# First attention of an eight-layer block: the first mixture's rows are gathered inside it

## The reference, cut to what matters

```python
x = x + mamba(layernorm(x))
x = x + ffn0(layernorm(x))      # mixture of 32 experts, 4 of them for each token
x = x + attn_b(layernorm(x))    # "rotary": 16 heads of 16, causal
x = x + ffn0(layernorm(x))
x = x + attn_sinks(layernorm(x))
x = x + ffn1(layernorm(x))      # mixture of 48 experts, 8 for each token
x = x + attn_latent(layernorm(x))
x = x + ffn1(layernorm(x))
```

```python
def ffn0(x):                    # its end
    outs = experts(x)[inverse_order].reshape(-1, 4, 256)
    return sum(outs * topk_weight[..., None], axis=1)

def attn_b(x):
    q, k, v = split(x @ w_atten.T)          # 16 heads of 16
    q, k = rope(q), rope(k)
    att = softmax(where(causal, q @ k.T / 4, -inf))
    return (att @ v) @ w_proj.T
```

## Time and profile before

| | us |
|---|---|
| median of 3 runs | 4055.43 |
| lowest and highest | 4052.91, 4055.51 |
| span of the profiled execution | 4055.4 |

### The profile page before, as it was taken

How to read it: one execution, slowest core, us unless ns; L and a number is a source line. 1 busy time by engine, 2 the same in 40 slices (tenths; PEclk the granted TensorE clock), 3 DMA queues, 4 the chain that set the end, 5 groups by cost and what they waited for, 6 DMA issues and landing times. The chain is left out here.

```text
span 4055.4 us, 68591 instructions
## 1 busy us (share of the span) xinstructions
PE 3283.2 (81%) x19700; PEld 2595.3 (64%) x19707; DVE 2809.6 (69%) x6227; ACT 2274.5 (56%) x5958; POOL 1766.8 (44%) x3039
## 2 busy tenths in 40 slices
PE   7799967925888489169999999999957499999575
PEld 3355556714777377058778778778745378888453
DVE  5699966646777666368858858768673378888742
ACT  3599923414777344068858868768602166666211
POOL 0299923567664045635535445446327400000165
PEclk9699977967999689579999999999956599999666
DMA  2011132440000335310000000000053500000435
GB/s 86 20 47 47 49 153 80 137 104 24 1 1 1 148 99 136 98 59 19 19 9 19 20 9 20 17 10 20 16 184 63 119 1 1 1 1 1 160 72 111
DMA packets 139453, 221.35 MB, mean 55 GB/s; under 512 B 28912, under 2 KB 114800, under 8 KB 137408
## 3 DMA queue, kind: packets, MB, share of 16 engines
q1 hardware_dynamic: 108432, 156.23, 11.6%
q0 software_dynamic: 30720, 61.44, 7.3%
HBM read 162.60 MB, written 54.80 MB: 54 GB/s over the span
## 5 line engine op out<-in xcount | busy, mean ns | idle before, releaser
L1242 POOL DMA_INDIRECT ex_xr<-scratch_rows,mo_token x288 | 287.0, 997 | 326.1 <-PE bank L1301 167.7
L596 POOL TENSOR_TENSOR sc_h<-sc_h,sc_c 128x512 f32<-128x512 f32 x256 | 327.0, 1291 | 198.1 <-DVE sc_h L633 190.1
L3034 DVE TENSOR_TENSOR sa_pT<-bank,sa_pT 128x512 fp32r<-128x512 f32 x512 | 329.9, 686 | 34.4 <-ACT sa_pT L2902 30.5
L2894 ACT ACTIVATE sa_p<-bank,sa_nm 128x512 f32<-128x512 f32 x512 | 347.0, 689 | 2.5 <-DVE sa_nm L3025 2.5
L633 DVE TENSOR_TENSOR_SCAN sc_h<-sc_da,bank 128x512 f32<-128x512 f32 x256 | 311.1, 1220 | 39.4 <-ACT sc_da L576 24.5
L2723 PE MATMUL bank<-sa_kT,sa_qT 128*128 128x512 f32 x1024 | 332.5, 436 | 1.5 <-DVE residual L3001 1.5
L3021 DVE TENSOR_REDUCE sa_mx<-bank 128x2 f32<-128x1024 f32 x256 | 312.4, 1220 | 25.7 <-PE bank L2725 22.0
L1319 PE MATMUL bank<-mo_w_gu,ex_xT 128*128 (+2 forms) x1152 | 315.7, 403 | 1.1 <-issue 0.5
L2747 PE MATMUL bank<-sa_pT,sa_v 128*128 128x256 f32 x2048 | 301.5, 290 | 16.9 <-DVE sa_pT L3034 16.5
L2747 PEld LDWEIGHTS bank<-sa_pT,sa_v 128*128 128x128 f32 x2048 | 260.2, 190 | 40.1 <-DVE sa_pT L3034 31.6
L2902 ACT ACTIVATE sa_pT<-bank 128x512 fp32r<-128x512 f32 x512 | 274.3, 585 | 7.9 <-PE bank L2735 0.7
(11 more groups left out here) (401 smaller groups left out, 9405.6 us busy)
## 6 DMA issues: line engine op xcount, KB each, us to landing
scratch_ys<-ex_yo SPq DMA_DIRECT2D x192, 128.0 KB, 2.1
mo_w_gu<-in_w_gu SPq DMA_DIRECT2D x2, 9216.0 KB, 26.8
sc_c<-scratch_c SPq DMA_DIRECT2D x64, 256.0 KB, 3.1
sa_share<-scratch_shares SPq DMA_DIRECT2D x256, 64.0 KB, 2.5
mo_w_dn<-in_w_dn SPq DMA_DIRECT2D x2, 4608.0 KB, 46.5
scratch_rows<-ln_stage SPq DMA_DIRECT2D x64, 128.0 KB, 1.9
mo_w_dn<-in_w_dn SPq DMA_DIRECT2D x2, 4096.0 KB, 34.8
ex_xr<-scratch_rows,mo_token POOLq DMA_INDIRECT x288, 2.8
```

The lines of the kernel that those rows point to most:

```text
L596: pool.tensor_tensor(h, h, C[u], ALU.mult).then_inc(used.sem, 1)
L1242: pool.indirect_dma_start(xr[u][:, :], None, rows, bass.IndirectOffsetOnAxis(ap=token[:, i:i + 1], axis=0), bounds_check=rows.shape[0] - 1 ...
L2894: act.activation(pr[h][:, :], SC[2 * s_ + h][:, :], ACT.Exp, bias=nm[:, col:col + 1], scale=SCALE, accum_out=rs[:, col:col + 1]).then_inc( ...
L3034: dve.tensor_tensor(spot(1), PT[h][:, :].rearrange("p (k n) -> p k n", k=TPB), spot(0).bitcast(F32), ALU.subtract).then_inc(*inc("kept_d"))
```

## The change

- After the first mixture there is no combine block. `slots` and `weights` are kept (`c.slots`, `c.weights`, in the scope `c.kept`) and `rotary` gathers and adds the rows itself. After the second mixture `combine(c)` runs as before, now as an entry of `LAYERS`.
- GpSimd, in the attention's block: first the 16 gathers of batch 0 (`fetch_rows`, 12 buffers `got`), then mask and identity, 8 gathers of batch 1, the rotation of all of group 1, the other 8 gathers of batch 1, and in the loop four gathers at the end of each of the groups 0 to 7.
- VectorE clears the `qT` parts (8 memsets) instead of GpSimd, then adds the 16 rows of batch 0, takes four statistics, and computes variance and deviation of batch 0 alone. In the loop it adds one row in each unit of group 0, one in every other unit of groups 3, 4, 7 and 8, and in groups 1, 5 and 9 it takes the next batch's statistics (`r` 0 to 3), its variance (`r` 3) and its deviation (`r` 6).
- VectorE rotates all four tiles of group 0, with `low_v(1, i)` after each; GpSimd none of them.
- ScalarE clears `vv` with four copies from zeros, and takes the root of batches 1 to 3 in the loop, at `r` 4 of groups 1, 5 and 9.

```diff
@@ rotary, GpSimd
+                fetch_rows(0, PB)
                 pool.memset(mask[:, :], 0.0).then_inc(*inc("made"))
...
-                for u in range(2):
-                    for hh in range(HG):
-                        rows = slice(WR, P) if hh % 2 == 0 else slice(0, WR)
-                        pool.wait_ge(*at("made", 4 + u * HG + hh))
-                        pool.memset(qT[u][rows, hh * SEQ:(hh + 1) * SEQ].bitcast(F32), 0.0).then_inc(*inc("made"))
-                for u in range(4):
-                    pool.memset(vv[u][:, :].bitcast(F32), 0.0).then_inc(*inc("made"))
-                pool.wait_ge(*at("made", 4 + 2 * HG + 4))
+                pool.wait_ge(*at("made", 4))
+                fetch_rows(PB, PB + 8)
...
-                put_group(0, (0, 1))
-                pool.sem_inc(sig["qput"].sem, 2)
+                pool.sem_inc(sig["qput"].sem, TPB)
                 put_group(1, range(TPB))
+                fetch_rows(PB + 8, 2 * PB)
                 for I in range(NG + 1):
...
+                    if 2 * PB + I * TPB < BATCH * PB:
+                        fetch_rows(2 * PB + I * TPB, 2 * PB + (I + 1) * TPB)
@@ rotary, TensorE
                     if I == 0:
-                        pe.wait_ge(*at("dput", 2))
+                        pe.wait_ge(*at("dput", TPB))
@@ rotary, ScalarE
+                for u in range(4):
+                    act.activation(vv[u][:, :].rearrange("p (o n) -> p o n", n=P),
+                                   blank.to_broadcast([P, TPB * HG + 1, P]), ACT.Copy).then_inc(v_cleared.sem, 1)
...
+                    if r == 4 and I % G == 1 and I // G + 1 < BATCH:
+                        take_root(I // G + 1)
@@ rotary, VectorE
+                def add_row(n):
+                    u, i = n % NB, n // K0
+                    at_x = c.x[:, i * D_MODEL:(i + 1) * D_MODEL]
+                    dve.wait_ge(fetched[u].sem, fetched[u].at(16 * (n // NB + 1)))
+                    if n % K0:
+                        dve.wait_ge(weighed.sem, weighed.at(n))
+                    dve.scalar_tensor_tensor(out=at_x, in0=got[:, u * D_MODEL:(u + 1) * D_MODEL],
+                                             scalar=c.weights[:, n:n + 1], in1=at_x,
+                                             op0=ALU.mult, op1=ALU.add).then_inc(weighed.sem, 1)
...
+                for i in range(TPB):
+                    for k in range(K0):
+                        add_row(i * K0 + k)
+                    if i >= 1:
+                        tile_stats(i - 1)
+                tile_stats(TPB - 1)
+                variance(0)
+                deviation(0)
...
-                for i in (2, 3):
+                for i in range(TPB):
                     dve.wait_ge(*at("qraw", i + 1))
                     st.then(put(dve, st, 0, i, scratch[1]))
                     dve.sem_inc(sig["dput"].sem, 1)
-                for i in range(TPB):
                     low_v(1, i)
...
+                    if I == 0:
+                        add_row(PB + r)
+                    if I % G in (3, 0) and r % 2 == 0 and PB <= (I + 1) // G * PB < (BATCH - 1) * PB:
+                        add_row(((I + 1) // G + 1) * PB + (I + 1) % G * (PB // 2) + r // 2)
+                    if I % G == 1 and I // G + 1 < BATCH:
+                        if r < TPB:
+                            tile_stats((I // G + 1) * TPB + r)
+                        if r == TPB - 1:
+                            variance(I // G + 1)
+                        if r == 6:
+                            deviation(I // G + 1)
@@ layers
-LAYERS = ["mamba", "moe0", "rotary", "moe0", "sinks", "moe1", "latent", "moe1"]
+LAYERS = ["mamba", "moe0", "rotary", "moe0", "combine", "sinks", "moe1", "latent", "moe1"]
```

More of the change, by code:

```diff
@@ L723, in moe @@
     TPBANK = TILES // EB
+    if which == 0:
+        keep = lambda name, dt: c.kept.enter_context(nc.sbuf_tensor(name, [P, TK], dt, allow_name_mangling=True))
+        c.slots, c.weights = keep("mo_slots", I32), keep("mo_weights", F32)
     with ExitStack() as s:
@@ L1091, in moe, with combine @@
             rowed[u].counted(16 * (TILES // 4))
[L1093 to L1097 removed]
+def combine(c):
     nc = c.nc
+    K, ROWS, ys, slots, weights = M0_K, M0_TILES * P, c.t["scratch_ys0"], c.slots, c.weights
     NB = 16
@@ L2096, in _, with fetch_rows @@
             def _(pool):
+                def fetch_rows(first, end):
+                    for n in range(first, end):
+                        u = n % NB
+                        if n >= NB:
+                            pool.wait_ge(weighed.sem, weighed.at(n - NB + 1))
+                        pool.indirect_dma_start(got[:, u * D_MODEL:(u + 1) * D_MODEL], None, ys,
+                                                bass.IndirectOffsetOnAxis(ap=c.slots[:, n:n + 1], axis=0),
+                                                bounds_check=ys.shape[0] - 1, oob_is_err=False) \
+                            .then_inc(fetched[u].sem, 16)
+                fetch_rows(0, PB)
                 pool.memset(mask[:, :], 0.0).then_inc(*inc("made"))
@@ L2380, in _ @@
-                st.then(dve.reciprocal(rstd[:, :], tmp[:, :]))
+                def add_row(n):
[7 more added lines that the diff above has]
+                                             op0=ALU.mult, op1=ALU.add).then_inc(weighed.sem, 1)
@@ new lines, in deviation @@
+                def deviation(b):
+                    cut = slice(b * TPB, (b + 1) * TPB)
+                    dve.wait_ge(*at("root", b + 1))
+                    st.then(dve.reciprocal(rstd[:, cut], tmp[:, cut]))
+                for u in range(2):
+                    for hh in range(HG):
+                        rows = slice(WR, P) if hh % 2 == 0 else slice(0, WR)
+                        dve.memset(qT[u][rows, hh * SEQ:(hh + 1) * SEQ].bitcast(F32), 0.0).then_inc(q_cleared.sem, 1)
+                for i in range(TPB):
[3 more added lines that the diff above has]
+                        tile_stats(i - 1)
@@ L2480, in rotary @@
             sig[n].counted(v)
+        for u in range(NB):
+            fetched[u].counted(16 * len(range(u, TILES * K0, NB)))
+        for q, v in ((weighed, TILES * K0), (q_cleared, 2 * HG), (v_cleared, 4)):
+            q.counted(v)
+    c.kept.close()
 def sinks(c):
```

61 lines of the change are left out of this document (36 added, 25 removed).

## The result

| | before | changed | ratio, 95% interval |
|---|---|---|---|
| median, us | 4055.47 | 4014.76 | 0.9896 (0.9882 to 0.9909) |
| lowest and highest of 4 runs | 4052.91, 4059.81 | 4010.83, 4016.94 | |
| span of the profiled execution | 4055.4 | 4008.8 | |

The account below looks back on a forecast made before the run. Gathers bound the combine, a VectorE chain the attention's start, VectorE-ScalarE hand-overs the loop. Saved 76.7, less 2.2 at the start and 30.2 in the loop, gives 44.3 us: 4055.4 to 4011 us, range 3996 to 4030.

Parts of the forecast that it names:

- What goes from the path: First gather to first normalized tile: 102.7 us shrinks to 26.0, saving 76.7 us.
- the clearing: Memsets moved to VectorE and ScalarE: first adds up to 2 or 3 us late, cost 0, at most 4.6 us.
- The start: Attention's start: VectorE's four rotations of group 0 delay the transposes by 3.7 us; net for this part 2.2 us.
- 1.5 back in group 0: Loop's group 0: TensorE's 1.49 us wait for GpSimd goes, as GpSimd starts group 1 earlier.
- one share, 0.78: Loop: 0.78 of 38.7 us added to VectorE and ScalarE is exposed, 30.2 us; ends 0.4 and 1.15.
- the added work is of the same kind and in the same places: Loop: the reason given for taking 0.78, from two groups differing by four normalizations, transposes and copies.
- The cost of 0: Loop: GpSimd's four gathers per group, 5.2 us, fit into its 8.1 us idle and cost nothing.
- its sign of being wrong: Loop: TensorE waiting for GpSimd's rotations would show the prediction wrong; no size given.
- A: Loop's idle time absorbs added work: 0.4 exposed or less, 3996 us or less, 3981 with nothing exposed; chance 0.08.
- B: Loop: more than all exposed through broken hand-overs, table loads and lower clock; 1.4 of 38.7, 4035 us; chance 0.08.
- C: Loop: slow gathers make GpSimd's rotations late; 4090 us at 4.5 us each, no gain above 3.4; chance 0.04.
- The two rules: Loop: a 1380 ns drain per table switch, 8.3 us over six, not counted; port lock, up to 3 us, put at nothing.

Follow-up runs that it names:

- e2_no_loop_rows: Changed kernel with the 48 gathers and 48 adds of batches 1 to 3 left out; 4003.71 us in one run.
- e1_copy_root: Changed kernel with ScalarE's square root of batches 1 to 3 replaced by a plain copy, so no table loads in the loop; 4004.09 us in one run.
- e12_no_variance: Changed kernel with the seven variance steps of batches 1 to 3 left out, mean 0 and variance 1 instead; 4005.66 us in one run.
- e7_newton: Changed kernel with loop adds moved into VectorE's waits and roots of batches 1 to 3 moved from ScalarE to VectorE and GpSimd; 4003.08 us, ratio 0.9872.
- e10_stats_placed: As e7_newton, with the loop's statistics put two and two ahead of the value copies of units 2 and 3; 3998.89 us, ratio 0.9863.
- e3_gathers_only: Changed kernel with the 48 adds of batches 1 to 3 left out but their 48 gathers made; 4001.95 us in one run.
- e11_stats_split: As e10_stats_placed, with GpSimd again rotating tiles 0 and 1 of group 0; 4011.67 us, ratio 0.9894.
- e8_pool_clears: Changed kernel with GpSimd again clearing both kinds of buffers, behind its first 16 gathers and the masks; 4021.7 us in one run.
- e9_changed_again: The changed kernel unaltered, run again on the chip of three other kernels; 4015.99 us, ratio 0.9902 against the kernel before.

## Why the prediction was right, and which steps failed

**What goes from the path: right.** 102.7 to 25.4 is 77.3 us; 76.7 was said. The gathers kept their pace, and nothing of the clearing, of the loads or of the tables added to it by the 16th add. The first adds were late by the 2 or 3 us that the prediction allowed, because the first row landed late, and not because of the clearing. The medians are those of the earlier trace rows; the longest gather took 1.18 us and the longest add 0.73:

```profile
L2113 POOL DMA_INDIRECT ra_got<-scratch_ys,mo_slots x64: 992/998/1176, 838.3 to 1107.2; - x64
L2403 DVE SCALAR_TENSOR_TENSOR residual<-ra_got,mo_weights,residual x64: 468/482/728, 843.5 to 1131.8; 128x256 f32<-128x256 f32 x64
...
DMA to landing us min/median/max: 2.7/2.8/5.2
```

**The start: a little short.** The forecast was 3.7 us later up to the first maximum, and 1.5 back in group 0. Measured: 4.6 and 5.3 later. VectorE's four rotations ran from 872.26 to 885.80 in the changed kernel, 13.5 us where 12.4 was said. (By the prediction's own numbers, 964.5 - 960.88, the first part is 3.6, not 3.7.) The 1.5 us did not come back although the wait for GpSimd in group 0 is gone: group 0 without its adds (e2_no_loop_rows) is 0.5 longer than before, not 1.5 shorter. Its first 4 us, and those of the kernel before:

```profile
892.20:896.20 4.00, 4.00 (x15) 3.49 (x15) 1.29 (x5) 2.63 (x10) 2.09 (x7) 0.50 0.01 4
```
```profile
966.00:970.00 4.00, 3.98 (x26) 3.16 (x25) 1.73 (x6) 2.78 (x11) 3.52 (x11) 1.00 0.02 4
```

TensorE is busy throughout in both, but does 15 matmuls at a granted clock of 0.50 in one and 26 at 1.00 in the other. It had stood idle for 5.7 to 6.1 us for the rotations. This cost of the longer wait stands in no step of the prediction. That it is what ate up the 1.5 us is the nearest reading; no run takes it away alone.

**The loop: the mechanism right, the share too small for one half of the work.** The sum has one share, 0.78, on 38.7 us: 30.2. With the 1.5 that was to come back the loop should have grown by 28.7; it grew by 35.9 and 37.3. By kind, from the runs:

| kind | added, us | cost of the loop, us | share |
|---|---|---|---|
| 48 adds | 19.9 | 15.2 to 15.6 | 0.76 to 0.78 |
| 6 table loads | 7.7 | 8.2 to 9.1 | 1.1 to 1.2 |
| 3 variances | 4.4 (5.9 measured) | 7.1 to 8.5 | 1.6 to 1.9 (1.2 to 1.4) |
| 48 gathers (GpSimd) | 62 of its time | 0.4 | 0 |
| the rest, not taken apart | 6.7 | 3 | 0.4 |

In the rows of loads and variances the lower cost counts groups 1, 5 and 9 alone. The kinds add up: in group 5 the loads make 2.8 us (e1_copy_root), the variance 2.6 (e12_no_variance) and the four statistics 1.3 (from e7_newton to e10_stats_placed), 6.7 together where the group took 6.6. The rest is 12 statistics, three reciprocals and three roots, together with what group 0 lost to the clock and won from the wait. The failing step is "the added work is of the same kind and in the same places". For the adds it was. The variance is seven dependent steps in one place ahead of one maximum, and the load holds up one exponential; such a block is longer than the wait that VectorE or ScalarE has in its one unit (1.4 us at most in the kernel before), so little of it is taken in, and TensorE runs at the lower clock behind it. A second step was mis-sized: the variance takes 1.98 us in the loop and not 1.46, 1.6 us over three batches. (Its 0.43 us for a statistic stands in no row shown, where the earlier trace rows give 0.49; it took 0.42.) The share was taken from normalizations that stand one to a unit, and must not be carried to a block.

**The gathers and GpSimd: right for the change, with less room than said.** The cost of 0 held, and its sign of being wrong, that TensorE waits for GpSimd's rotations, did not occur: the two waits that the profile puts down to GpSimd were for ScalarE's copy. The expectation of e3_gathers_only, too, takes them for GpSimd's. But two rotations more on GpSimd turned it into the bound of group 1 (e11_stats_split).

**The rivals.** A, nothing exposed, fell: 35.9 us came back. What speaks for a part of it is that placement gets most of the adds' cost back. B, more than all exposed by broken hand-overs and a falling clock, is what the loads and the variances show, 15.3 to 17.6 us of the 35.9, but not the adds; at 0.93 over all it came out well short of 1.4. C did not occur: the median gather took 0.998 us, the longest 1.18.

**The two rules.** Behind each of the two loads shown above the activation starts at once (1036.37 + 1.28 = 1037.65, root at 1037.66; 1038.85 + 1.28 = 1040.13, exponential at 1040.14). The Trainium skill (ScalarE: Activation LUTs, What ACT_TABLE_LOAD costs) has 2.66 us for a switch; the trace shows 1.28, and by the run without loads a switch costs 8.2 / 6 to 9.1 / 6, or 1.4 to 1.5 us, knock-on included. The Trainium skill's other rule, the exclusive lock on the shared ports (SBUF — State Buffer, Who interferes with whom), the trace bears out for a memset against VectorE's operations from SBUF to SBUF, in the earlier trace rows and in e8_pool_clears. The prediction put its effect in the loop at nothing. There the seven steps took 1.98 us and not 1.46: five of them ran 0.24 to 0.38 us beside GpSimd's rotation, where in the changed kernel's start all took 0.16 to 0.17. That fits the rule, but the runs do not part a lock from other delays, so up to 0.5 us of it per batch stays open.

**What stays open.** On the chip of the second comparison the medians differ by 4052.2 - 4015.99 = 36.2 us, where the expectation of e9_changed_again had 41; the first comparison's 40.7 is the high one of the two. They exceed the savings of their stages, 37.1 and 34.9, by 3.6 and 1.3 us. The part behind the attention was shorter in the changed kernel's two traces (by 7.3 and 3.6 us) and in most others, yet longer by 0.2 and 0.8 in e2_no_loop_rows and e11_stats_split; and the first gather came 2.1 and 1.0 us sooner than before, in other traces up to 3.3 us sooner or at the same time. With a single trace of the kernel before, whether these are its own scatter was not settled.

## What to carry to other kernels

Work that is moved off a serial prologue into a loop whose engines hand work to each other comes back with a price set by its place: about 0.8 of itself if strewn one piece to a unit, little if each piece stands where its engine waits anyway (eight adds here cost 0.4 to 1.0 us in groups 3, 4, 7 and 8, of 3.3 us of work), and more than all of itself if it is a dependent block ahead of one hand-over, or a table load. Size each kind by a row of its own shape, and add the lower clock that TensorE shows behind an idle stretch. An engine with much idle time (GpSimd here) can still be the bound of one group, so count its room group by group before giving it more. And where a wait names an engine that had long been done, look for the other wait of the same instruction: twice it was ScalarE here and not GpSimd.

## What the runs showed of the hardware beyond that

- TensorE's granted clock was 0.61 in the 3.5 us behind an idle time of 1.99 us in group 5 and 0.50 in the 4.1 us after them, and 0.50 for the first 4 us of group 0 in e2_no_loop_rows behind an idle time of 6.1 us and some 5 us of work. Four transposes took 1.09 us at the lower level and 0.60 to 0.63 at the upper.
- VectorE's operations on 128x256 elements from SBUF to SBUF waited for GpSimd's memsets (6.51 us for four, 1.38 without), while in the combine of before its adds ran at 0.48 us beside indirect gathers of 0.99 to 1.01 us, 64 of 64. With other work beside them, the longest add took 0.73 us and the longest gather 1.18.
- An indirect gather of 128 rows of 1 KB landed 2.8 us after its issue (median), the first one of the changed kernel after 5.2 us.
- ScalarE cleared the four value buffers, 128x2176 elements each, in 7.74 us, about GpSimd's 7.46, beside the gathers, where nothing else was due on it.
